# Mixture-of-experts tail on one core: neighbouring spare blocks write to separate rows, and the last block's up product is issued earlier

## The reference

```python
logits = jnp.einsum('bsh,eh->bse', x, gate_w)          # 8 experts
top_w, top_i = jax.lax.top_k(softmax(logits), 2)       # 2 experts per token
g = x @ w_gate[e];  u = x @ w_up[e]                    # 512 -> 352, per expert
h = silu(g) * u
expert_out = h @ w_down[e]                             # 352 -> 512
out = x + sum over the 2 chosen experts of weight * expert_out
        + sigmoid(x @ shared_gate_w) * ((silu(x @ sw_gate) * (x @ sw_up)) @ sw_down)
```

## Time and profile before

| | us |
|---|---|
| median of 3 runs | 689.49 (689.24 to 690.12) |
| the profiled execution's own time | 687.42 |
| its span, first to last instruction | 685.7 |
| PE busy | 652.5 (95%) |
| DVE busy | 300.5 (44%) |
| ACT busy | 228.6 (33%) |
| POOL busy | 161.0 (23%) |
| mean granted TensorE clock | 0.987 of full speed |

### The profile page before, as it was taken

How to read it: one execution, slowest core, us unless ns; L and a number is a source line. 1 busy time by engine, 2 the same in 40 slices (tenths; PEclk the granted TensorE clock), 3 DMA queues, 4 the chain that set the end, 5 groups by cost and what they waited for, 6 DMA issues and landing times.

```text
span 685.7 us, 10319 instructions
## 1 busy us (share of the span) xinstructions
PE 652.5 (95%) x3426; PEld 332.2 (48%) x3426; DVE 300.5 (44%) x703; ACT 228.6 (33%) x341; POOL 161.0 (23%) x134
## 2 busy tenths in 40 slices
PE   8889999999999999999999799999999999999990
PEld 5544444444444444444444344455555555555550
DVE  3899554525524445523559763452222222222220
ACT  3445053313710223620345353332223222223220
POOL 2560280005000004000435700013222222222221
PEclk9999999999999999999999999999999999999995
DMA  9531097222420314430367987348888888888852
GB/s 279 182 92 47 12 307 224 85 93 110 101 39 0 63 32 156 96 60 0 61 210 264 282 276 169 105 117 128 131 128 132 134 129 135 135 126 139 122 72 31
DMA packets 146899, 85.77 MB, mean 125 GB/s; under 512 B 109721, under 2 KB 131481, under 8 KB 146850
## 3 DMA queue, kind: packets, MB, share of 16 engines
q1 hardware_dynamic: 134722, 56.25, 36.0%
q0 software_dynamic: 10544, 27.30, 17.9%
q10 hardware_dynamic: 1584, 1.57, 0.7%
HBM read 32.76 MB, written 27.29 MB: 88 GB/s over the span
## 4 chain that ended last, share of the span: by engine, by line
PE 70%; issue 10%; DMA 7%; DVE 7%; SPq 1%; POOLq 1%; ACT 1%; POOL 1%; ACTq 0%
PE bank L1593 30%; PE bank L1608 16%; PE bank L1641 9%; PE bank L1668 6%; PE bank L1450 5%; DMA out<-staging,token_blk 4%; DMA hidden<-hT 2%; PE bank L1407 2%; DMA arena<-x 1%; PE bank L1416 1%; POOLq L652 1%; DVE arena L955 1%; DVE stats L936 1%; DVE arena L1287 1%; POOL out L657 1%
## 5 line engine op out<-in xcount | busy, mean ns | idle before, releaser
L1593 PE MATMUL bank<-hT,arena 128*128 128x512 f16 x1056 | 238.0, 379 | 5.7 <-DVE prod L1313 4.8
L1593 PEld LDWEIGHTS bank<-hT,arena 128*128 128x128 bf16 x1056 | 102.5, 98 | 132.0 <-DVE prod L1313 6.2
L1641 PE MATMUL bank<-arena,hx_odd 128*128 x936 | 146.0, 313 | 0.0
L1608 PE MATMUL bank<-arena,hidden 128*128 128x512 bf16 x528 | 120.3, 379 | 0.0
L1641 PEld LDWEIGHTS bank<-arena,hx_odd 128*128 128x128 f16 x936 | 91.1, 98 | 53.8 <-issue 0.9
L657 POOL DMA_INDIRECT out<-staging,token_blk x39 | 60.8, 1558 | 165.1 <-ACT staging L913 139.0
L1350 DVE TENSOR_TENSOR prod<-silu_sb,bank 128x352 f32<-128x352 f32 x39 | 20.3, 521 | 150.7 <-PE bank L1641 150.7
L1668 PE MATMUL bank<-arena,hidden 128*128 (+1 forms) x351 | 82.3, 379 | 4.1 <-DMA hidden<-hT 2.5
L1608 PEld LDWEIGHTS bank<-arena,hidden 128*128 128x128 bf16 x528 | 51.3, 98 | 63.0 <-issue 2.3
L875 ACT ACTIVATE silu_sb<-bank 128x512 f32<-128x512 f32 x44 | 26.2, 596 | 112.1 <-PE bank L1593 112.0
L1313 DVE TENSOR_TENSOR prod<-silu_sb,bank 128x512 f32<-128x512 f32 x44 | 30.1, 684 | 75.4 <-PE bank L1593 71.3
(11 more groups left out here) (190 smaller groups left out, 506.3 us busy)
## 6 DMA issues: line engine op xcount, KB each, us to landing
staging<-L_ffn_w_gate SPq DMA_DIRECT2D x6, 704.0 KB, 4.9
staging<-L_ffn_w_up SPq DMA_DIRECT2D x6, 704.0 KB, 5.9
arena<-x SPq DMA_DIRECT2D x3, 1024.0 KB, 7.4
out<-arena POOLq DMA_DIRECT2D x3, 1024.0 KB, 4.8
staging<-L_ffn_w_down SPq DMA_DIRECT2D x6, 512.0 KB, 3.8
staging<-L_ffn_sw_gate SPq DMA_DIRECT2D x11, 256.0 KB, 3.3
staging<-L_ffn_sw_up SPq DMA_DIRECT2D x11, 256.0 KB, 3.9
staging<-L_ffn_sw_down SPq DMA_DIRECT2D x11, 256.0 KB, 4.5
```

What stands on the lines that cost most here:

```text
L1593: op = nc.tensor.matmul(ps[:, :], weights[:, j, wp, kind, c * P:(c + 1) * P], hT[:, t % 2, hp, c, :], start=(c == 0 and s == 0), stop=(c = ...
L1608: op = nc.tensor.matmul(out_ps[i][:, :], hidden[:, j % 3, hp, i * P:(i + 1) * P], weights[:, j, wp, DOWN, :], start=(j == 0 and s == 0), s ...
L1641: op = nc.tensor.matmul(ps[:, 0:I], xT[:, k % X_SLOTS, xp * KC + c, :], arena[:, bass.ds(at + (part_at(0, part) + wp * low_gap(part) + c * ...
```

## The change

There are two edits.

1. Spare places alternate between two sets of 128 rows behind the real ones. The spare places with odd number get the row number `NT + P + p` in their last four columns; this needs a small tile `pad_odd`, and two DMAs in place of one for each of the three odd places. The output gets 128 more rows, zeroed by one more DMA. The table adds `ended[k-1]`, which is 1 where block k-1 is a spare one, to `same_expert[k]`, so that a spare block behind a spare block has its count lowered by 16 too.
2. UP(38) moves ahead of DOWN(36), and the turn of block 38 moves ahead of DOWN(37). PE's order at the end becomes UP(37), GATE(38), UP(38), DOWN(36), turn of 38, DOWN(37), DOWN(38). ACT does `last_hidden_high` ahead of `weigh(37)`.

```diff
+    SPARE_FILLS = NBLK - MIN_BLK + (NBLK - MIN_BLK) // 2
...
+                nc.gpsimd.tensor_scalar(pad_odd[:, :], pad_id[:, :].broadcast_to([P, XW - TOKEN]), P, None,
+                                        ALU.add).then_inc(pad_ready, 1)
...
-                pool.wait_ge(pad_ready, 1)
+                pool.wait_ge(pad_ready, 2)
                 for n in range(NBLK - MIN_BLK):
-                    pool.dma_start(xs_dram[SPARE + n * P:SPARE + (n + 1) * P, :],
-                                   pad_row[:, :]).then_inc(spare_filled, 16)
+                    spare = xs_dram[SPARE + n * P:SPARE + (n + 1) * P, :]
+                    if n % 2:
+                        pool.dma_start(spare[:, 0:TOKEN], pad_row[:, 0:TOKEN]).then_inc(spare_filled, 16)
+                        pool.dma_start(spare[:, TOKEN:XW], pad_odd[:, :]).then_inc(spare_filled, 16)
+                    else:
+                        pool.dma_start(spare, pad_row[:, :]).then_inc(spare_filled, 16)
...
-            pool.dma_start(out[NT:NT + P, :], pad_row[:, 0:H]).then_inc(spare_filled, 16)
+            for n in range(2):
+                pool.dma_start(out[NT + n * P:NT + (n + 1) * P, :], pad_row[:, 0:H]).then_inc(spare_filled, 16)
...
-            pool.wait_ge(spare_filled, 16 * (NBLK - MIN_BLK + 1))
+            pool.wait_ge(spare_filled, 16 * (SPARE_FILLS + 2))
...
                     weigh(k - 1)
+            last_hidden_high()
             weigh(NBLK - 2)
-            last_hidden_high()
             weigh(NBLK - 1)
...
+                    nc.vector.tensor_tensor(same_place[:, 1:NBLK], same_expert[:, 1:NBLK], ended[:, 0:NBLK - 1, E - 1],
+                                            ALU.add)
...
-                    nc.vector.scalar_tensor_tensor(out=table[:, 3, 1:NBLK], in0=same_expert[:, 1:NBLK], scalar=-16.0,
+                    nc.vector.scalar_tensor_tensor(out=table[:, 3, 1:NBLK], in0=same_place[:, 1:NBLK], scalar=-16.0,
...
-                expert_product(k, UP, at).then_inc(eu_done, 1)
+                if k < NBLK - 1:
+                    expert_product(k, UP, at).then_inc(eu_done, 1)
+                else:
+                    turn_last_hidden()
                 if k + 1 < NBLK:
                     at = block_gate(k + 1)
+                if k == NBLK - 2:
+                    pe.wait_ge(ep_ready, k)
+                    expert_product(k + 1, UP, at).then_inc(eu_done, 1)
                 if k == 1:
                     pe.wait_ge(piece_low_dve, PIECES - POOL_LOW)
                 if k > 0:
                     expert_down(k - 1, down_from)
                 down_from = pe.value_load(table[0:1, 2, k:k + 1], min_val=0, max_val=(E - 1) * 2 * DN)
-            turn_last_hidden()
             expert_down(NBLK - 1, down_from)
```

More of the change, by code:

```diff
@@ L328, in build_xattn_moe @@
         pad_id = sb("pad_id", [P, 1], I32)
+        pad_odd = sb("pad_odd", [P, XW - TOKEN], F32)
         count = sb("count", [P, E], F32)
@@ L343, in build_xattn_moe @@
         same_expert = sb("same_expert", [P, NBLK], F32)
+        same_place = sb("same_place", [P, NBLK], F32)
         pad_full = sb("pad_full", [P, E], F32)
@@ L546, in _ @@
             sp.wait_ge(table_ready, 1)
-            sp.wait_ge(spare_filled, 16 * (NBLK - MIN_BLK))
+            sp.wait_ge(spare_filled, 16 * SPARE_FILLS)
             for b in range(B):
@@ L1724 @@
     n_tokens, n_experts = shape[0] * shape[1], inputs["L0_ffn_w_gate"].shape[0]
-    out = nc.dram_tensor("out", (n_tokens + P, shape[2]), F32, kind="ExternalOutput").ap()
+    out = nc.dram_tensor("out", (n_tokens + 2 * P, shape[2]), F32, kind="ExternalOutput").ap()
     xs_rows = n_experts * n_tokens + (n_experts - 1) * P + n_experts * P
```

## The result

The changed kernel takes 686.03 us (median of 9 runs, 684.82 to 687.78), before takes 689.38 us (9 runs, 685.22 to 690.55). The ratio is 0.996 with a 95% interval of 0.9942 to 0.9977: 1.6 to 4.0 us faster, 2.8 by the ratio itself, with the medians 3.35 us apart. Forecast were 685.9 us and a gain of 3.6. The profiled execution took 685.29 us with a span of 683.6.

What follows compares the result with a forecast made beforehand. The prediction took the spare blocks' adds, waiting in line, to bound the end, and PE nearly everything before. It summed -3.7 + 0.1 = -3.6 us, 689.49 to 685.9 us, range 684.9 to 688.0.

Steps and rivals of the forecast that it cites:

- The bound: Last 12 us: adds of 36, 37 and 38 stand in line, some 5.6 us apart; PE's work doesn't set the end.
- The table: Counts for 37 and 38 drop by 16; with this edit alone 38's add starts 3.5 to 3.7 us sooner.
- UP(38) moved: Ahead of DOWN(36) it takes 1.79 us of PE, so 36's add starts later, at 664.5 to 664.75 us.
- The meeting at the buffer: `weigh(38)` waits for 36's add to land, 669.2 to 669.6 us; the last add starts at 670.2 to 670.8.
- rival 2: At block 38's buffer: 36's add lands before 667.9, so no wait; 5.3 us gained, 684.3 us; chance 0.05.
- term -3.7: At the kernel's end: the last add starts at 670.5 instead of 674.17 us, 3.7 us gained.
- The operation on DVE: One more table sum ahead of PE's 3.49 us wait near 383 us: costs 0.1 to 0.2 us, taken as 0.1.
- The fills: Four more DMAs on POOL, 2.2 to 2.5 us, ahead of `send_rows(0)`; over 60 us of cover, cost taken as 0.
- rival 4: Extra fills on POOL reach the critical path, costing 2.5 us: 688.4 us; chance 0.06.
- Rivals 1 and 3: Last adds: 1, overlapping adds slow each other, 688.0 us, chance 0.08; 3, adds stay in line, 691.3 us, chance 0.05.
- Rival 3: Last adds stay in line because the table's value doesn't free them: +1.7 and 0.1, 691.3 us; chance 0.05.

Runs made afterwards that it cites:

- the order alone: Kernel before with only the new order of PE and ScalarE, its spare rows and table unchanged: 690.93 us, ratio 1.003 to before.
- the spare rows alone: Full change with PE's and ScalarE's order taken back to that of before, keeping two spare row sets and the table: 686.67 us, ratio 0.9969 to before.
- the additions ahead alone: Kernel before plus the change's extra fills, `pad_odd` and the table operation with its result unused; order as before: ratio 1.0004 to before.
- the own buffer: Full change plus a third set of spare rows and a buffer only block 38 uses: 688.92 us, ratio 0.9969 to before.

## Why the prediction was right

**The bound.** That the adds stand in line and PE doesn't set the end was right: the order alone took PE's 1.50 us of idle time away and made the kernel slower, and the spare rows alone gave the gain.

**The table.** Right. By the sum 37 and 38 no longer wait for the add in front: in the change 37's starts 2.54 us behind 36's, and 36's landing hasn't come by then.

**UP(38) moved.** Forecast 664.5 to 664.75 for the add of 36 where before had 662.96, so 7.1 to 7.35 us behind block 35's; measured 7.14.

**The meeting at the buffer.** Forecast that block 38 would be ready for weighing 1.3 to 1.7 us before it may be, that the last add would start at 670.2 to 670.8, 12.8 to 13.4 us behind block 35's; measured 1.2 us and 13.03. Two small misses cancel in this: 36's add landed 4.45 us after its start and not after 4.67 to 4.83, and from the weighed block 38 to its add it took 0.65 us and not 0.27 to 0.49. POOL's wait for that same landing stands in the code ahead of its reading of the table for 38, which could make the step longer, but no run isolates it. With a buffer of its own it started 1.46 us sooner. The row on the landing (4.67 to 4.83 us) was the one to go by, and rival 2 is out. By the Trainium skill's page "DMA: Bandwidth & Descriptors", section "Anatomy of one DMA — SWDGE (gpsimd) path", the estimate was 2.6 us; the trace disagrees, with 4.45 us for 36's landing.

**The size.** The last add came 3.74 us sooner between the first two profiles, but the change is worth somewhat less. From block 35's add to the end, the five profiles with the adds in line and PE's old order have 28.30, 27.67, 27.94, 28.00 and 27.98 us, mean 27.98; the two with the change's end have 24.76 and 24.63, mean 24.70. That is 3.3 us. The term -3.7 was read from one execution whose adds happened to be 5.6 us apart, where the other four have mostly 5.3 to 5.5. With 0.1 for the table it gives 3.2, beside 3.35 between the medians and 2.8 by the ratio. So the mechanism was right and its size 0.4 us too large; that the median of the runs came within 0.2 us of the forecast 685.9 is luck in part, with the gain known only as 1.6 to 4.0.

**The operation on DVE.** PE's wait at 383 us went from 3.49 to 3.63 us, 0.14, inside the forecast 0.1 to 0.2. It is 3.63 or 3.64 in all five profiles that have the operation and this wait, and 3.49 or 3.50 in all four without it. No timing here resolves it. In saying what hangs on this wait I left out the clock: as many as eight profiles lose 1.7 us or more behind it. That changed nothing in the difference, since before loses it too in two of its three profiles.

**The fills.** Fills and output's zeros took 6.95 us on POOL (84.83 to 91.78) where before had 4.83, 2.1 more, and ACT's copy for sequence 2 started at 171.73 us, as late against the store at 150.46 us as before (21.3 us in both). Nothing waits; rival 4 is out.

**Rivals 1 and 3.** The landing of 36 wasn't late in the change (4.45 us), though 37's add was in flight. In the four profiles where the last two adds start 1.86 us apart the last landing took 4.7 to 5.3 us, against 4.6 alone, so the mechanism can cost up to 0.7, not 2.1. Rival 3, a table that frees nothing, is what the order alone shows: 1.4 us later from block 35's add to the end (29.36 against 27.98), forecast +1.7.

## What to carry to other kernels

When a chain of completions sets the end, filling the idle time of the busiest engine changes nothing, and moving its work forward can delay the very completion that the chain waits for: count from the event that starts the last chain, and ask of each moved step whose result it pushes back. Spare or padding work that is kept for a fixed shape should not share a destination, or it serialises what is otherwise free. Where the executions of two kernels differ by some microseconds ahead of the place of the change, compare both from a mark just in front of it, and over several profiles, before a term is sized from one.

## What the runs showed of the hardware that was not expected

A wait of TensorE of 3.5 to 3.6 us was followed by a granted clock at its half level in eight of nine profiles, for 3.4 us in most and, in two (the additions ahead alone, the own buffer), for 6.4 us or more by the windows from 383 to 390 us; a wait of 1.2 us at the same place never was, in four profiles. Shortening it by 2.3 us on before brought 4.5 us (2.8 to 6.3), nearly twice its length; on the change it brought 4.3, known to some 2 us either way. Two accumulating indirect DMAs of 256 KB that start 1.86 us apart both land, the second after 4.7 to 5.3 us rather than 4.5 to 4.8 where they start 2.5 to 3.8 us apart.
